# A decoder layer on one core: new steady orders on four engines in the attention step, the attention output transposed a step later, cross maxima and subtraction one PSUM bank at a time

## What is computed

```python
def _L0_attn_ref(x, Wv, bv, Wo, bo):                 # 16 heads of 8 features
    p = jnp.einsum('bsd,ed->bse', x, Wv) + bv        # q = k = v = p, split into heads
    scores = jnp.einsum('bhqd,bhkd->bhqk', q, k) / math.sqrt(dk)
    out = jnp.einsum('bhqk,bhkd->bhqd', jax.nn.softmax(scores, axis=-1), v)
    ...
    return jnp.einsum('bsd,ed->bse', out, Wo) + bo
def _L0_xattn_ref(querys, keys, values):             # the same heads, no projections
    ...
x = x + _L0_attn_ref(_layernorm(x), Wv, bv, Wo, bo)
x = x + _L0_xattn_ref(_layernorm(x), ctx_1024, ctx_1024)
x = x + _L0_ffn_ref(_layernorm(x), ...)
```

## Time and profile before

| what | us |
|---|---|
| median of three runs | 415.33 |
| span of the profiled execution, first to last instruction | 427.0 |
| first transposes of step 5 to those of step 32 (27 steps) | 33.26 to 226.85 |
| step 32 | 226.85 to 233.96 |
| tail of the attention phase, up to the last turn of unit 30 | 233.96 to 251.08 |

### The profile page before, as it was taken

One profiled execution on the slowest core, in us unless ns is written; L12 is line 12 of the kernel. 1 busy time (PEld: TensorE's weight loads), 2 busy tenths in 40 slices (PEclk: granted clock), 3 DMA queues, 4 the chain that ended last, 5 costly groups with the idle time before them and its releaser, 6 DMA issues.

```text
span 427.0 us, 16199 instructions
## 1 busy us (share of the span) xinstructions
PE 404.4 (95%) x5545; PEld 312.9 (73%) x5546; DVE 305.1 (71%) x791; ACT 298.5 (70%) x684; POOL 284.8 (67%) x476
## 2 busy tenths in 40 slices
PE   7989999999998999999999898969999999999997
PEld 4646666666665666666665667959988999999996
DVE  7868999999998998999999787713333444444444
ACT  7659999999998999999998685302213466666651
POOL 8757788878887888888888423665664463444442
PEclk9999999999999999999999999996999999999999
DMA  6254566767676667765444300021113255430001
GB/s 104 43 85 64 87 103 108 109 110 121 120 124 117 114 123 126 143 101 84 60 63 43 35 2 2 27 81 58 69 69 90 67 133 139 131 104 27 27 32 52
DMA packets 176324, 35.22 MB, mean 82 GB/s; under 512 B 145587, under 2 KB 174646, under 8 KB 176256
## 3 DMA queue, kind: packets, MB, share of 16 engines
q1 hardware_dynamic: 71296, 21.43, 23.1%
q10 hardware_dynamic: 102144, 6.81, 15.2%
q0 software_dynamic: 2816, 6.10, 4.1%
HBM read 20.86 MB, written 15.67 MB: 86 GB/s over the span
## 4 chain that ended last, share of the span: by engine, by line
PE 68%; DMA 10%; issue 6%; DVE 6%; ACT 3%; SPq 2%; POOL 2%; another core or an unknown queue 2%; DVEq 0%; ACTq 0%; POOLq 0%
PE psum L867 15%; PE psum L659 12%; PE psum L668 12%; PE psum L973 8%; PE psum L680 7%; DMA orow<-attention_out 3%; DMA attention_out<-on_s 3%; PE psum L690 3%; SPq L198 2%; DMA ring<-sorted_rows 2%; PE psum L763 2%; PE psum L802 2%; PE psum L758 1%; PE psum L809 1%
## 5 line engine op out<-in xcount | busy, mean ns | idle before, releaser
L1583 DVE TENSOR_TENSOR gT<-gT,psum 128x384 f32<-128x384 f32 x66 | 36.5, 553 | 77.5 <-PE psum L867 34.4
L1263 ACT ACTIVATE gT<-psum 128x384 f32<-128x384 f32 x70 | 33.6, 488 | 58.4 <-PE psum L867 36.9
L620 POOL DMA_INDIRECT out<-yrow,token x38 | 37.1, 975 | 41.2 <-DVE yrow L1718 22.0
L973 PE MATMUL psum<-wdn_sb,gT 128*128 (+1 forms) x420 | 60.2, 280 | 4.0 <-DVE rows_all L1597 2.2
L479 POOL TENSOR_TENSOR k_s<-pT,hmask_sb 128x1024 f32<-128x1024 f32 x32 | 61.0, 1906 | 0.9 <-ACT pT L1137 0.8
L973 PEld LDWEIGHTS psum<-wdn_sb,gT 128*128 128x128 f32 x420 | 53.3, 195 | 5.7 <-issue 2.7
L867 PE MATMUL psum<-fhT,wtile 128*128 128x128 f32 x456 | 57.2, 275 | 0.3 <-ACT wtile L1292 0.3
L867 PE MATMUL psum<-hT_all,wup_sb 128*128 128x128 f32 x384 | 50.9, 283 | 5.0 <-issue 3.8
L867 PEld LDWEIGHTS psum<-fhT,wtile 128*128 128x128 f32 x456 | 53.9, 192 | 0.5 <-ACT wtile L1292 0.5
L867 PEld LDWEIGHTS psum<-hT_all,wup_sb 128*128 128x128 f32 x384 | 47.7, 198 | 6.0 <-issue 4.8
L1065 ACT ACTIVATE pr_x<-pr_x,rs 128x512 f32<-128x512 f32 x60 | 43.0, 722 | 8.2 <-DVE pr_x L1368 7.0
(11 more groups left out here) (193 smaller groups left out, 872.0 us busy)
## 6 DMA issues: line engine op xcount, KB each, us to landing
sorted_rows<-nowhere_row SPq DMA_DIRECT2D x38, 130.0 KB, 3.6
ring<-sorted_rows SPq DMA_DIRECT2D x30, 130.0 KB
wup_sb<-in_wup SPq DMA_DIRECT2D x14, 176.0 KB, 3.0
orow<-attention_out SPq DMA_DIRECT2D x31, 64.0 KB
ring<-in_ctxv ACTq DMA_DIRECT2D x60, 32.0 KB, 3.7
cross_keys<-in_ctxk ACTq DMA_DIRECT2D x14, 128.0 KB, 3.7
ring<-cross_keys SPq DMA_DIRECT2D x112, 16.0 KB
rows_all<-in_x ACTq DMA_DIRECT2D x10, 128.0 KB, 3.9
```

The costliest lines, as they stand in the source:

```text
L620: pool.indirect_dma_start(out=out, out_offset=bass.IndirectOffsetOnAxis(ap=token[p][:, 0:1], axis=0), in_=yrow[p][:, :], in_offset=None, b ...
L973: last = nc.tensor.matmul(ps_y[p], gT[place_of(n) if isinstance(n, int) and n < FIRST else p][:, c, :], wdn_sb[:, expert, c, :], start=(c ...
```

## The change

It reorders the bodies of four engines. Nothing is computed in another way, except that the cross maxima and the cross subtraction become two instructions each, one for each PSUM bank.

- TensorE: `turn_output` moves from the end of step n+3 to step n+4, between the two halves of `turn("s")`. `project` moves between the two halves of `weigh("s")`, the transpose of `xn_p` between the two halves of `turn("x")`, `cross_weighed` 0 ahead of the projections, and `cross_weighed` 1 ahead of `cross_scores`. In the tail one `turn_output(U - 3)` comes between the two turns of unit 31.
- VectorE: from step 5 on, the moments of the incoming rows and of `st_x` come behind the softening of s. `invert` and `normalise("s")` come ahead of it. The cross maxima and subtraction are split. The tail is as before.
- ScalarE: from step 4 on, the copy `v_s` comes behind the second `prT_s`; `onT` comes between the two `prT_s`, and `xnT` between the two `prT_x`.
- GpSimd: from step 4 on `k_s` is the first of a step; `xn_s` and its variance come ahead of `xb` and of the addition of `on_x`.

```diff
@@ GpSimd body
+                late = t >= LAG["q"]
+                if live("proj") and late:
+                    keys_masked(u["proj"])          # k_s, the old lines as a function
...
+                if live("q"):
+                    ...xn_s, then ve (the old lines)
                 if live("xb"):
                     ...
@@ TensorE body
                 if live("soft_s"):
                     turn("s", u["soft_s"], 0)
+                if live("q"):
+                    turn_output(u["q"])
+                if live("soft_s"):
                     turn("s", u["soft_s"], 1)
-                if live("q"):
-                    project(u["q"])
...
                     weigh("s", u["soft_s"], 0, v_s[u["soft_s"] % 2][:])
+                if live("q"):
+                    project(u["q"])
+                if live("soft_s"):
                     weigh("s", u["soft_s"], 1, v_s[u["soft_s"] % 2][:])
...
                 if live("pv_x"):
-                    cross_weighed(u["pv_x"], (0,))
+                    cross_weighed(u["pv_x"], (1,))
                 if live("q"):
                     cross_scores(u["q"])
-                if live("pv_x"):
-                    cross_weighed(u["pv_x"], (1,))
-                if live("out"):
-                    turn_output(u["out"])
@@ TensorE tail
             turn("s", U - 1, 0)
+            turn_output(U - 3)
             turn("s", U - 1, 1)
@@ ScalarE body
+                if live("proj") and t >= LAG["q"]:
+                    values_out(u["proj"])           # v_s, the old lines as a function
                 bulk_of_step(t)
@@ VectorE body
+            def maximum_of(k, u, g):
+
+                dve.wait_ge(sem(f"{k}_sc"), at(u))
+                nc.vector.tensor_reduce(mx[k][:, g, :], scores_of(k, g), AX.X, ALU.max).then_inc(sem(f"{k}_mx"), 1)
...
-                    maxima("x", u["pv_x"])
-                if live("pv_x"):
-                    soften_both("x", u["pv_x"])
+                    maximum_of("x", u["pv_x"], 0)
+                    maximum_of("x", u["pv_x"], 1)
+                    soften("x", u["pv_x"], 0)
+                    soften("x", u["pv_x"], 1)
```

More of the change, by code:

```diff
@@ L796, in body @@
                     query(u["q"])
+                if live("pv_x"):
+                    cross_weighed(u["pv_x"], (0,))
                 if live("xT"):
@@ L1128, in output, with values_out @@
                 nc.scalar.copy(onT[:], ps_oT).then_inc(sem("s_onT"), 1)
+            def values_out(u):
+                if u >= 2:
+                    act.wait_ge(sem("s_pv"), G * (u - 1))
+                act.wait_ge(sem("p_pv"), at(u))
+                for h2 in range(2):
+                    rows = slice(S * h2, S * (h2 + 1))
+                    last = nc.scalar.copy(v_s[u % 2][rows, :].rearrange("p (a b e) -> p b a e", a=HP, b=NB)[:, :, :, DK * h2:DK * (h2 + 1)],
+                                          ps_v[rows, :].rearrange("p (b a d) -> p b a d", a=HP, b=NB))
+                last.then_inc(sem("p_v"), 1)
             def body(t, u, live):
@@ L1137, in body @@
                     nc.scalar.activation(pT[:], ps_pT, ACT.Identity, bias=bv_sb[:, 0:1]).then_inc(sem("p_pT"), 1)
[L1138 to L1145 removed]
+                if live("proj") and t < LAG["q"]:
+                    values_out(u["proj"])
                 if live("soft_s"):
```

108 lines of the change are left out of this document (52 added, 56 removed).

## The result

The changed kernel takes 417.06 us (median of six runs, 415.98 to 417.63), the kernel before 415.56 us (six runs beside them, 414.82 to 415.93). The ratio is 1.004, with a 95% interval of 1.0024 to 1.0056: slower by 1.5 us, where 414.4 was predicted. The measured 417.06 lies near the upper end of the range given. The profiled execution has a span of 415.6 us.

The account below looks back on a forecast made before the run. TensorE was taken as the bound, with no idle in a typical 7.07 us step. The terms -1.1 - 1.2 - 0.1 + 1.5 = -0.9 us took 415.33 to 414.4 us; range 411.4 to 417.3.

Parts of the forecast that it names:

- typical step: Steps 5 to 32: 7.03 us instead of 7.07, -1.1 us over 27 steps; ends -2.7 and +2.2.
- DMA waits and long steps: Steady steps: waits of the `orow` transpose for its DMA shrink from 2.1 to 0.9, -1.2 us; ends 0 and -2.1.
- prologue: Steps 4 and 5: one delay of 0.3 and one help of 0.4, -0.1 us, between -0.5 and +0.5.
- tail: From step 32: `st_x` starts at 5.18 instead of 3.68, behind GpSimd's later addition, +1.5 us; ends +0.8 and +2.0.
- `on_s` ahead of `pr_s`: VectorE's order in step 4: delays one softening by 0.3 us.
- `v_s` out of the way: ScalarE in step 5: the copy no longer stands ahead of exp s, which helps by 0.4 us.
- The modes: TensorE's steady step: eight changes of tiling mode instead of seven, +0.10 us a step.
- the vanished waits of turn x and `qT`: TensorE's steady step: waits of 0.11 for the second cross exponential and 0.03 behind `qT` go.
- the tightest place I named, `qT`: ScalarE's copy ahead of the cross scores: ready at 6.00 against 5.99 asked by TensorE, no slack.
- `prT_s` 0 (1.36 against 1.35): ScalarE's copy ahead of the first `weigh` s: ready at 1.36, TensorE asks at 1.35; the other place without slack.
- slower: the `qT` path: Rival: ScalarE's run from `prT_x` 0 to `qT` ends late every step, 7.15 a step, 418.0 us; chance 0.19.
- The split: VectorE's cross maxima and subtraction: four halves at 2.40 cost nothing; rival that they pay twice, 417.8 us, chance 0.02.

Follow-up runs that it names:

- the store on SyncE: Changed kernel, but SyncE issues both halves of the store of `on_s` up to step 32: 415.44 us, ratio 1.0007 to the kernel before.
- the fillers: Changed kernel plus four matmuls behind the projections of step 3 that only keep TensorE busy: 415.86 us, ratio 1.0019 to the kernel before.
- The second prologue run: Changed kernel, but in steps 0 to 3 the transpose of `xn_p` and its copy `xnT` have their old places: 416.01 us, ratio 1.0028.
- all mendings: Changed kernel with the tail mended, old prologue order in steps 0 to 3, the store on SyncE and the fillers: 424.96 us, ratio 0.9931.
- the run with `on_s` late: Changed kernel, but from step 5 on `on_s` is written behind the two halves of `pr_s`: 428.31 us, ratio 1.0006 to the kernel before.
- the store moved 0.8 later: Changed kernel, but ScalarE issues its store of `on_s` behind `prT_s` 0 instead of ahead of `oT_x`: 419.85 us, ratio 1.0133.
- the last run: Kernel before, with cross maxima and subtraction split, `turn_output` a step later and `project` behind turn_back x: 427.83 us, ratio 0.9998.
- without the split: Changed kernel with all mendings, but cross maxima and subtraction one instruction each in attention steps: 433.59 us, ratio 1.0102 to the kernel before.
- the tail mended: Changed kernel, but in GpSimd's last body (step 32) the addition of `on_x` stands ahead of `xn_s`: 415.32 us, ratio 1.0014.
- the last four variants: All mendings, the same without the split, the run with `on_s` late, and the last run: 424.96, 433.59, 428.31 and 427.83 us.

## Why the prediction was wrong

| term | predicted | in the traces |
|---|---|---|
| typical step, x 27 | -1.1 | +1.1 (7.11 instead of 7.07) |
| DMA waits and long steps | -1.2 | -2.4 (excess 2.7, now 0.3) |
| prologue | -0.1 | +1.4 (34.67 instead of 33.26) |
| tail | +1.5 | +1.4 (8.54 instead of 7.11) |
| sum | -0.9 | +1.5 |

These are the terms at full clock: 34.67 is where step 5 begins in the two traces that have the changed prologue and no half clock, with the store on SyncE and with the fillers. The times at full clock agree with the sum. The run with the fillers has it in all twelve executions, 415.86 us; the 15 executions of the kernel before beside it that have it take 414.40, 1.46 less. In the changed kernel's own profile the prologue reads +2.95 and the sum +3.05: 0.39 of the further 1.54 is there when step 3 begins, and 1.16 is step 4, at half clock (7.93 instead of 6.77).

Two terms failed: the prologue, by 1.5 us, and the typical step, by 2.2, of which the DMA term gave back 1.2.

**The prologue.** I costed "`on_s` ahead of `pr_s`" and "`v_s` out of the way", found -0.1 between -0.5 and +0.5, and left out the moved transpose of `xn_p` with its copy `xnT`, because I laid the new order over a steady step alone. Outside steps 5 to 31 the same code is another order. With this one term at +1.4 the sum would have been +0.6: no gain. The second prologue run shows the cause, and in its trace the size; the time fell by 0.5 us only.

**The typical step** was forecast as 7.03 and is 7.11. The modes, `project`'s 0.42, the vanished waits of turn x and `qT` all came as laid out (one sum of mine doesn't add up: the terms given for ScalarE between the second exponential of s and the first of x make 2.76, not 2.6; the trace with all mendings has 2.61), and the tightest place I named, `qT`, holds. It failed at the second one, "`prT_s` 0 (1.36 against 1.35)": I counted the end of the exponential and not the 0.61 us of the store's issue behind it, though the text itself moved that store to -0.2. The rival "slower: the `qT` path" foresaw a lateness of this kind (0.08 a step came) on the wrong path. Removing the issue gives 7.04, 0.01 from the forecast; so does `on_s` in its old place.

**DMA waits.** The size was off in our favour: I left a wait of 0.9 and the scattered excess as it was; both went. That the ScalarE half decides the round trip is borne out by the run with `on_s` late (one wait of 0.9), and by the store moved 0.8 later, which brought three back. The later place of `turn_output` helps by itself: the last run, with `on_s` where it was, had one wait in its steps. These are single traces of each, and such waits differ between executions.

**The tail** was right in mechanism and size (1.69 of waiting, +1.43, last `orow` at 15.03).

**The split** was costed at nothing and called a risk at most. It is the best part of the change: 0.06 us a step in the old order, 0.26 in the new. The rule of the Trainium skill that I set against it (VectorE: DVE Perf Modes, "The TRN2 errata") doesn't decide here. The Trainium skill asks there for tiles of at least 512 elements, and the halves have just that. In the trace a half takes 0.60 start to start and a whole 1.2, and the halves let ScalarE begin sooner.

The profile before, 427.0 us, was long behind the attention phase: 175.9 us from the last turn of unit 30 to its end, against 161.5 in the profile after. The terms above are all from the attention phase and add up, at full clock, to the measured difference, so taking the difference unscaled did no harm here.

## What to carry to other kernels

An order that is written once for all steps of a software pipeline has to be laid out for its first and last steps too: name, for each line that moves, its neighbours when half the stages aren't live. A DMA issue cost ScalarE nothing here only where the next operation was held by something else; look at when the issue *ends*, not where it stands. And work put in a hole that another engine leaves costs only what sticks out of the hole (0.17 of `project`'s 0.42 us), while moving it away can make the step longer (by 0.25). Single executions differ in their clock by as much as such a change is worth, so compare those with the same clock.

## What the hardware showed beside

- The issue of a store of `on_s` or of a load into `ring` takes 0.61 to 0.64 us of ScalarE in the rows above, and where the next operation is ready it begins 0.10 behind the issue's end, while otherwise it begins 0.10 before the last one's end. It can be issued before the operation ahead of it in the program has begun: at 98.62 against 98.72 with `on_s` behind `pr_s`. But it isn't issued while that one still waits for its input: at 109.93, when `pr_x` was ready, without the split. Once, in the run with the store moved, the issue of a load took 1.61 us, and the exponential behind it waited 1.00 us.
- The half clock after the idle of step 3 comes in some executions and not in others of the same kernel: with the tail mended, six of twelve have a mean clock of 0.995 or 0.996, and their median is 416.39 us, against 414.93 for the other six, 1.5 us less. In the traces step 4 lasts 7.93 and 8.30 us with it and 6.77 without. The four fillers (eight records, 2.00 us in all) ended it in all twelve executions.
- Beside the last four variants the kernel before took 427.96 us instead of 414.9, and they were slower likewise. In their traces it all lies behind the attention phase, in the routing and the experts (173.0 us from the last turn of unit 30 with all mendings, 161.5 with the store on SyncE). TensorE has seven waits there that the profile puts down to issue, 4.4 us in all, and 3.4 us at half the granted clock. The profile before, with its 427.0 us, is of the same kind: five such waits, 3.8 us, and 6.8 us at half clock. What sets this isn't known.
